# Routing stage of a fused attention and mixture-of-experts block: rows and their weights stored apart, in other queues

## What is computed

```python
x = _L0_conv_ref(x, ...)
t = _to_tokens(x)
t = t + _L1_attn_ref(_ln_t(t), ...)
t = t + _L1_ffn_ref(_ln_t(t), ...)      # the part in question
# _L1_ffn_ref: 4096 tokens of 256, 8 experts with 1024 hidden, 2 experts for each token
gate_logits = x_flat @ gate_w.T
topk_vals, topk_idx = jax.lax.top_k(gate_logits, 2)
topk_w = softmax(topk_vals)
out = sum over e of comb[:, e] * (gelu(x_flat @ w1[e].T + b1[e]) @ w2[e].T + b2[e])
```

## Time and profile before

| | us |
|---|---|
| median of 3 runs | 1495.16 (1491.56 to 1496.29) |
| the profiled execution | 1490.46 |
| its span, first to last instruction | 1488.6 |
| granted TensorE clock, mean over the span | 0.912 of full |
| PE busy | 1214.1 (82%) |
| DVE / ACT / POOL busy | 792.0 / 696.3 / 548.2 |
| the route begins (first DMA of the stage) | 916.2 |
| slots known | 1012.4 |
| first matmul of the experts | 1022.2 |

### The profile page before, as it was taken

How to read it: one execution, slowest core, us unless ns; L and a number is a source line. 1 busy time by engine, 2 the same in 40 slices (tenths; PEclk the granted TensorE clock), 3 DMA queues, 4 the chain that set the end, 5 groups by cost and what they waited for, 6 DMA issues and landing times. The chain is left out here.

```text
span 1488.6 us, 27970 instructions
## 1 busy us (share of the span) xinstructions
PE 1214.1 (82%) x9389; PEld 817.3 (55%) x9390; DVE 792.0 (53%) x1573; ACT 696.3 (47%) x1344; POOL 548.2 (37%) x452
## 2 busy tenths in 40 slices
PE   3989989833997798779887987345999999999993
PEld 1546756621334444433443345345888888888882
DVE  3855655445465756566657345464454454454441
ACT  3565544436578567756775743233323323323321
POOL 3977555211900280044000001002555656656641
PEclk7989999966999899989999997557999999999996
DMA  4755889824960695089209604943443443444437
GB/s 169 172 140 140 179 171 191 185 78 78 243 190 1 127 255 156 1 163 248 71 1 185 184 1 149 416 125 87 66 72 66 76 71 69 74 71 71 75 53 240
DMA packets 330185, 190.22 MB, mean 128 GB/s; under 512 B 273712, under 2 KB 310832, under 8 KB 327920
## 3 DMA queue, kind: packets, MB, share of 16 engines
q1 hardware_dynamic: 292880, 129.30, 36.4%
q0 software_dynamic: 24704, 54.34, 16.3%
q10 hardware_dynamic: 12512, 5.41, 1.4%
HBM read 64.85 MB, written 60.96 MB: 85 GB/s over the span
## 5 line engine op out<-in xcount | busy, mean ns | idle before, releaser
L2108 ACT ACTIVATE all_last_rows<-moe_hbank,moe_b1T 128x256 f32<-128x256 f32 x312 | 130.0, 471 | 287.9 <-PE moe_hbank L2019 265.4
L2019 PE MATMUL moe_hbank<-moe_rowT,l_w1T 128*128 128x256 f16 x1872 | 213.1, 274 | 26.4 <-DMA moe_rowT<-moe_ends 26.3
L2019 PEld LDWEIGHTS moe_hbank<-moe_rowT,l_w1T 128*128 x1872 | 181.4, 98 | 56.5 <-issue 34.3
L2034 PE MATMUL moe_ybank<-l_w2T,moe_shared 128*128 x1872 | 210.6, 273 | 0.0
L2034 PEld LDWEIGHTS moe_ybank<-l_w2T,moe_shared 128*128 128x128 f16 x1872 | 183.0, 98 | 21.5 <-issue 0.3
L1175 ACT ACTIVATE block_probs<-block_bank 128x1024 f32<-128x1024 f32 (+1 forms) x192 | 144.5, 808 | 74.3 <-PE block_bank L937 62.2
L2287 DVE TENSOR_SCALAR moe_shared<-all_last_rows 128x2048 f16<-128x2048 f32 x39 | 48.3, 1239 | 219.5 <-ACT all_last_rows L2108 219.5
L1948 POOL DMA_INDIRECT acc_scratch<-moe_ends,moe_which x78 | 128.1, 1643 | 54.8 <-DVE moe_ends L2302 24.7
L804 POOL COPY block_stack<-block_stack 128x512 f16<-128x512 f16 x16 | 10.6, 662 | 362.3 <-ACT block_stack L1159 362.3
L934 PE MATMUL block_bank<-block_qkT 128*128 128x512 f16 (+3 forms) x384 | 94.9, 335 | 46.1 <-issue 24.4
L300 POOL TENSOR_SCALAR front_raw<-front_raw 128x1024 f32<-128x1024 f32 x32 | 92.0, 2874 | 55.2 <-ACT conv_probs L525 54.9
(11 more groups left out here) (364 smaller groups left out, 2463.2 us busy)
## 6 DMA issues: line engine op xcount, KB each, us to landing
front_raw<-in_L_ffn_w POOLq DMA_DIRECT2D x32, 512.0 KB, 5.4
w_turned<-block_qk SPq DMA_DIRECT2D x32, 512.0 KB, 3.6
w_parts<-front_raw_hi POOLq DMA_DIRECT2D x32, 256.0 KB, 5.5
w_parts<-front_raw_lo POOLq DMA_DIRECT2D x32, 256.0 KB, 5.9
l_w1T<-w_turned SPq DMA_DIRECT2D x8, 1024.0 KB, 18.4
l_w2T<-w_turned SPq DMA_DIRECT2D x8, 1024.0 KB, 20.0
rows_scratch<-moe_ends ACTq DMA_DIRECT2D x4, 1056.0 KB, 6.8
front_shared<-in_x SPq DMA_DIRECT2D x8, 512.0 KB, 6.4
```

What stands on the lines that cost most here:

```text
L2019: last = pe.matmul(hbank[:, c, :], w1T[:, e, wp, k, c * P:(c + 1) * P], rowT[q][:, xp * CC + k, :], start=n == 0, stop=n == 5)
L2034: last = pe.matmul(ybank[q][:, t, :], (hid_hi, hid_lo)[hp][q][:, c, t * P:(t + 1) * P], w2T[:, e, wp, c, :], start=n == 0, stop=n == 3 * H ...
L2108: act.activation(hid[:, c, :], hbank[:, c, :], ACT.Gelu, bias=b1T[:, e, c:c + 1], scale=1.0 / (GAIN * GAIN)).then_inc(S["gelu_done"], 1)
```

## The change

The row buffers hold 512 half words a row instead of 528. The tails of all 32 tiles live in a tile of their own, `extra`. Rows are stored by SP, each turn's once `x_lo` is there, and ahead of further expert weights; `xrow` needs no weights any more. ACT stores only the tails, 32 bytes a row, at the places where it stored the rows (`store_extra`). `token_weights` no longer waits for a store, and POOL waits for the tails too.

```diff
@@ -1751,9 +1751,10 @@
         hot = shared[:, :].bitcast(F16)
         in_col = [hot[:, i * PICKS * P:(i + 1) * PICKS * P].rearrange("p (n q) -> p n q", n=PICKS) for i in range(2)]
         of_col = [hot[:, (2 * P + i * COLS) * PICKS:(2 * P + (i + 1) * COLS) * PICKS].rearrange("p (n q) -> p n q", n=PICKS) for i in range(2)]
-        ends = s.sb("ends", [P, 2 * PER * ROW], F16)
-        xrow = [ends[:, i * PER * ROW:(i + 1) * PER * ROW].rearrange("p (t r) -> p t r", t=PER) for i in range(2)]
-        fields = [x[:, :, 2 * D:2 * D + 8].bitcast(F32) for x in xrow]
+        ends = s.sb("ends", [P, 2 * PER * 2 * D], F16)
+        xrow = [ends[:, i * PER * 2 * D:(i + 1) * PER * 2 * D].rearrange("p (t r) -> p t r", t=PER) for i in range(2)]
+        extra = s.sb("extra", [P, TILES, ROW - 2 * D], F16)
+        fields = [extra[:, a * PER:(a + 1) * PER, 0:8].bitcast(F32) for a in range(TURNS)]
         got = [ends[:, i * GT * ROW:(i + 1) * GT * ROW].rearrange("p (t r) -> p t r", t=GT) for i in range(4)]
         got_fields = [g[:, :, 2 * D:2 * D + 8].bitcast(F32) for g in got]
         y = [ends[:, 4 * GT * ROW + i * 2 * GT * D:4 * GT * ROW + (i + 1) * 2 * GT * D].bitcast(F32).rearrange("p (t d) -> p t d", t=GT) for i in range(2)]
@@ -1804,7 +1805,7 @@
         lbank, pbank = (hbank[:, c, 0:PER * E_N].rearrange("p (t e) -> p t e", e=E_N) for c in (6, 4))
         cbank, table = hbank[:, 2, 0:E_N], hbank[:, 0, 0:COLS]
-                 "var_done", "root_done", "rstd_done", "x_done", "x_hi", "x_lo", "x_stored0", "x_stored1", "blank_stored",
+                 "var_done", "root_done", "rstd_done", "x_done", "x_hi", "x_lo", "x_stored0", "x_stored1", "blank_stored", "extra_stored",
@@ -1814,7 +1815,7 @@
         t2_v = t2.rearrange("(a t p) d -> a p t d", p=P, t=PER)
         rows_v = rows.rearrange("(a p) r -> a p r", p=P)
         batch = (B - 1, *range(B - 1))
-        CONSTS, NARROWED = 13 + TURNS, 3
+        CONSTS, NARROWED = 12 + TURNS, 3
         KEYED, WHOLE = 4, 1.5 * 2.0 ** 23
 
         def all_tiles(eng, step, apart=0):
@@ -1850,24 +1851,26 @@
                     sp.dma_start(w1T[:, e, :, :, :].rearrange("p a k h -> p a (k h)"), w1_turned[e]).then_inc(w_loaded, 16)
                     sp.dma_start(w2T[:, e, :, :, :].rearrange("p a k d -> p a (k d)"), w2_turned[e]).then_inc(w_loaded, 16)
 
+                def store_rows(a):
+                    sp.wait_ge(S["x_lo"], a + 1)
+                    sp.dma_start(rows_v[batch[a] * PER:(batch[a] + 1) * PER, :, 0:D].rearrange("t p r -> p t r"), xrow[a % 2][:, :, :].bitcast(U32)).then_inc(S[f"x_stored{a % 2}"], 16)
+
                 load_tok(1)
                 sp.wait_ge(S["x_done"], PER)
                 sp.wait_ge(last_stored, 16 * PER // 2)
                 load_tok(2)
-                load_weights(0)
-                load_weights(1)
-                sp.wait_ge(S["x_lo"], 1)
+                store_rows(0)
                 sp.wait_ge(S["xT_full"], PER)
                 load_tok(3)
-                load_weights(2)
-                load_weights(3)
-                load_weights(4)
-                load_weights(5)
-                load_weights(6)
-                load_weights(7)
+                load_weights(0)
                 sp.wait_ge(S["consts"], CONSTS)
                 for t in range(GT):
                     sp.dma_start(rows_v[TILES + t], blank[:, :].bitcast(U32)).then_inc(S["blank_stored"], 16)
+                for a in range(1, TURNS):
+                    store_rows(a)
+                    load_weights(a)
+                for e in range(TURNS, E_N):
+                    load_weights(e)
 
                 def step(j, r):
                     q = r % 2
@@ -1898,10 +1901,9 @@
                 pool.memset(all_ones[:, :], 1.0).then_inc(S["consts"], 1)
                 pool.memset(sofar[:, 0, :], 0.0).then_inc(S["consts"], 1)
                 pool.memset(blank[:, :], 0.0).then_inc(S["consts"], 1)
-                for q in range(2):
-                    pool.memset(xrow[q][:, :, 2 * D:ROW], 0.0).then_inc(S["consts"], 1)
+                pool.memset(extra[:, :, :], 0.0).then_inc(S["consts"], 1)
                 pool.iota(iota_e[:, :], pattern=[[1, E_N]], base=0, channel_multiplier=0, allow_small_or_imprecise_dtypes=True).then_inc(S["consts"], 1)
-                pool.wait_ge(S["consts"], 7)
+                pool.wait_ge(S["consts"], 6)
                 pool.affine_select(out=before[:, :], in_=before[:, :], compare_op=ALU.is_gt, fill=0.0, base=0,
                                    pattern=[[1, P]], channel_multiplier=-1).then_inc(S["consts"], 1)
                 pool.iota(iota_t[:, :], pattern=[[GS, REGION]], base=0, channel_multiplier=0, allow_small_or_imprecise_dtypes=True).then_inc(S["consts"], 1)
@@ -1928,6 +1930,7 @@
                 pool.wait_ge(S["slots_known"], 2)
                 for q in range(2):
                     pool.wait_ge(S[f"x_stored{q}"], 16 * TURNS // 2)
+                pool.wait_ge(S["extra_stored"], 16 * TURNS)
                 pool.wait_ge(S["blank_stored"], 16 * GT)
                 for j in range(AHEAD):
                     gather(j, j)
@@ -2058,10 +2061,10 @@
 
-                def store_rows(a):
-                    act.wait_ge(S["x_lo"], a + 1)
+                def store_extra(a):
                     act.wait_ge(S["weights_set"], 3 * (a + 1))
-                    act.dma_start(rows_v[batch[a] * PER:(batch[a] + 1) * PER].rearrange("t p r -> p t r"), xrow[a % 2][:, :, :].bitcast(U32)).then_inc(S[f"x_stored{a % 2}"], 16)
+                    act.dma_start(rows_v[batch[a] * PER:(batch[a] + 1) * PER, :, D:ROW // 2].rearrange("t p r -> p t r"),
+                                  extra[:, a * PER:(a + 1) * PER, :].bitcast(U32), allow_slow_non_contiguous=True).then_inc(S["extra_stored"], 16)
 
                 def exps(a):
                     act.wait_ge(S["choice_kept"], 2 * (a + 1))
@@ -2075,7 +2078,7 @@
                         if a and i == 4:
                             exps(a - 1)
                         if a and i == 6:
-                            store_rows(a - 1)
+                            store_extra(a - 1)
                         act.wait_ge(S["xT_full"], a * PER + i + 1)
                         if a or i > 1:
                             act.wait_ge(S["logit_full"], a * PER + i - 1)
@@ -2094,7 +2097,7 @@
                         last = act.activation(picks, picks, ACT.Copy, scale=token_f[:, a * PER + i:a * PER + i + 1])
                     last.then_inc(S["col_valued"], 1)
                     if a == 0:
-                        store_rows(TURNS - 1)
+                        store_extra(TURNS - 1)
                 act.wait_ge(S["slots_known"], 2)
                 act.dma_start(b2r, b2.rearrange("(a e) d -> a e d", a=1).to_broadcast((P, E_N, D))).then_inc(S["bias_loaded"], 16)
                 act.wait_ge(S["bias_loaded"], 32)
@@ -2161,16 +2164,13 @@
                     dve.wait_ge(S["sofar_done"], a + 1)
 
                 def token_weights(a):
-                    q = a % 2
-                    if a >= 2:
-                        dve.wait_ge(S[f"x_stored{q}"], 16)
                     dve.wait_ge(S["exp_done"], a + 1)
                     dve.tensor_scalar(diff[:, :], ratio[:, :], 1.0, None, ALU.add).then_inc(S["ratio_done"], 1)
                     dve.wait_ge(S["ratio_done"], a + 1)
-                    dve.reciprocal(fields[q][:, :, 0], diff[:, :]).then_inc(S["weights_set"], 1)
+                    dve.reciprocal(fields[a][:, :, 0], diff[:, :]).then_inc(S["weights_set"], 1)
                     dve.wait_ge(S["weights_set"], 3 * a + 1)
-                    dve.tensor_tensor(fields[q][:, :, 1], ratio[:, :], fields[q][:, :, 0], ALU.mult).then_inc(S["weights_set"], 1)
-                    dve.tensor_copy(fields[q][:, :, 2], idxf[:, :, 0]).then_inc(S["weights_set"], 1)
+                    dve.tensor_tensor(fields[a][:, :, 1], ratio[:, :], fields[a][:, :, 0], ALU.mult).then_inc(S["weights_set"], 1)
+                    dve.tensor_copy(fields[a][:, :, 2], idxf[:, :, 0]).then_inc(S["weights_set"], 1)
                     dve.wait_ge(S["weights_set"], 3 * a + 3)
 
                 def keep_prefix(a):
```

## The result

The changed kernel takes 1487.34 us (median of 13 runs, 1484.60 to 1498.46), the kernel before 1496.39 (median of 13, 1491.56 to 1500.12). The medians lie 9.05 us apart; the ratio, near that of the means (1488.3 and 1496.4), is 0.9946 (95% interval 0.9928 to 0.9963): 8.1 us, or 0.54%, are gained, half of the 16.0 that were forecast. 1487.34 lies within the range given, but only because that range took in the rivals too. The gain forecast is wrong: the second rival came true, with the gain of 8 that it names.

The account below looks back on a forecast made before the run. ACT's 23.5 us of waits for row stores were taken to bound the route. 21.9 us gained on the path less 5.9 for late tails gave 16.0, from 1495.16 to 1479.2 us, range 1472 to 1490.

Parts of the forecast that it names:

- the second rival: ACT held issuing turn 3's tails or the bias: slots about 1004 or 1007, gain 8 or 5, 1487 to 1490; chance 0.17.
- What bounds the kernel: Route, 916 to 963: ACT waits 23.5 us in all for row stores to land before rewriting a row buffer.
- What the path gains: Route turns 2 and 3: without both waits, slots come 21.9 us earlier, at 990.5 instead of 1012.4.
- Clock: TensorE in the route: the granted clock stays at 0.50, the lower level.
- Weights in SP's queue: Five experts' weights behind turn 3's rows land by 987.5; TensorE needs them at 1000.3, 11 us or more of cover.
- Tails in ACT's queue: Before POOL's first gather: turn 3's tails, queued behind the bias, land at 996.4, 5.9 us after the slots.
- The price of a small write: Turn 3's tails in ACT's queue: 49 ns a packet, 3.1 us taken; 0.6 us by the bias packet's 9 ns.
- the first: Tails and bias in ACT's queue pass in few turns, never late: 21.9 us gained, 1473.3; chance 0.18.
- The third: Tail writes of 32 bytes very dear: no path gain at 0.30 us each, 1504.8 at 0.45 us; chance 0.15.
- The rule of the Trainium skill: DMA queues: engines go round rings by 9 to 17 descriptors, letting small tails through in a few turns, against the count.

Follow-up runs that it names:

- e7: e1 with the weights of experts 1 to 7 put ahead of the stores of turns 1 to 3 in SP's queue; one execution, 1502.16 us.
- e1: Changed kernel with ACT's load of the first bias issued before the route instead of after the last exponential; 1476.34 us, ratio 0.9892 to the kernel before.
- e3: Changed kernel with the bias load at its place but as 128 pieces of 256 bytes instead of 8192 of 4; one execution, 1477.87 us.
- e4: Changed kernel with the bias load at its place, cut into eight DMAs of one expert each; one execution, 1492.49 us.
- e2: Kernel before with only the bias load moved ahead of the route; 1504.84 us, ratio 1.0087 to the kernel before.

## Why the prediction was wrong

- *What bounds the kernel:* right. The 23.5 us at the row buffer were the price, and e7 brings a wait of 26.9 us back by the order of SP's queue alone.
- *What the path gains:* right in place and in cause, 22.05 us where 21.9 were forecast, with L2090 of turn 2 at R + 26.1 where 26.05 was forecast, and DVE late next as worked out. e1 has its slots at R + 74.2, forecast 74.3.
- *Clock:* right, 0.51 from 925.73 to 973.00, the lower level, as before.
- *Weights in SP's queue:* a few us late, without effect. The last of them landed at R + 75.2, where 987.5, that is R + 71.3, was forecast; the first matmul came at R + 97.6.
- *Tails in ACT's queue:* the count by packets is right (24.9 us for the tails of turn 2, 24.2 forecast, of which 19.7 were turns), and so is the end of it: the tails of turn 3 landed at R + 79.1, where 996.4, that is R + 80.2, was forecast. POOL waited for them no longer, because the slots were later still. **This part holds the step that failed.** "Behind the bias stands the tail of turn 3, issued at 998.70 - 21.9 = 976.8": I let the issue go through in 0.4 us and charged the bias to POOL's wait for the landing, 5.9 us. The queue does not take it. The bias, which I charged with nothing on ACT, holds the engine at its next issue, here 16.86 us, with three of four rounds of ACT, PE and DVE behind it. The slots come 13.7 us later than without (87.9 against 74.2), and 22.05 - 13.7 leaves the 8.3 us that the profile shows.
- *The price of a small write:* 49 ns a packet was taken, 8 ns measured, the lower end. By itself it would have moved the forecast by 2.5 us; on the path it was worth nothing, because nobody waited for the landing.
- *Rivals:* the first (small packets slip through) is refuted by 222 against 221 packets for the tails and 115 against 114 for the bias. The second was right in place, cause and size, "slots come at about 1004, gain 8": 1004 is R + 87.8, and it was 87.9. The 0.1 us is luck in part: ACT was let go 1.4 us later than the 992.1 worked out, and what followed took 10.7 us and not 12. I gave it 0.17 because SP had been held with ten DMAs and not with three; e3 and e4 show that DMAs were the wrong thing to count. My own sum had 512 packets an engine, against some 80 of SP's (ten DMAs of 128 packets over 16 engines) when it was held, and that comparison speaks for the hold. The third fell with the 8 ns.
- *The rule of the Trainium skill* (DMA: Bandwidth & Descriptors, Queues, rings and completion order: turns by packets of typically 9 to 17 descriptors) does not describe this trace. Even counts over 4 us alone would fit turns of equal bursts as well; but from 986.0 to 986.3, about the time of one turn on each of the 16 engines, the two queues moved 21 packets each, and 15 and 16 from 994.0 to 994.3, so that each element of 32 or 4 bytes takes a turn of its own. The measurement decides.

## What to carry to other kernels

Count a transfer that shares the DMA engines with large ones by its packets: beside packets of 8 KB each of its own cost a turn of about 0.3 us here, be it 4 bytes or 1 KB, and it costs it to everything behind it in its queue too. When a change brings an issue forward into a stretch where another queue is full, look at what it is then queued behind and at the engine that issues the next one: here the hold landed there and showed in no wait on a semaphore, only as a long issue. A load that was harmless where nothing ran beside it, as the bias before, has to be placed anew with the change.

## What the runs showed of the hardware

- An issue that follows 8192 outstanding packets on its queue, with SP's queue full of weights beside it, held the issuing engine 16.86 and 16.61 us in two runs; with the same bytes in 128 pieces it took 0.37 us.
- Where both had packets under way, two queues shared the engines packet for packet: 222 to 221 with 32 bytes against 8 KB, 115 to 114 with 4 bytes, 214 to 214 with 4 bytes in e2, 208 to 207 with 1 KB in the kernel before. A transfer may start late: the tails of turn 2, issued at 968.97, moved no packet until 973.4, while SP's queue moved rows of 1 KB, 275 packets from 971 to 972. Why is open.
- With nothing beside them, writes of 32 bytes to device memory ran at 8 ns of an engine each, no dearer than reads of 4 bytes (9 ns).
- A small early load can cost much later: in e2 a bias of 32 KB, issued at R, lengthened by 12.3 us the wait for a row store issued 22 us after it.
